# GpSimd sums x and the normalised rows at the end of layer 0's experts, where VectorE did it in layer 1's mix

## What is computed

```
x = x + experts0(layernorm(x))            # end of layer 0: the stage "mlp0"
xn = layernorm(x)
x = x + graph1(xn, edges) + mix1(xn)      # layer 1
# mix1: att = linear attention over xn (8 heads)
#       x1  = layernorm(xn + att @ Wo + bo)
#       out = layernorm(x1 + relu(x1 @ W1 + b1) @ W2 + b2)
# graph1(xn) ends with  "... + xn"
```

## Time and profile before

| what | value |
|---|---|
| time, median of 3 runs | 7430.36 us (7419.84 to 7437.67) |
| the profiled execution: its own time | 7422.03 us |
| its span | 7420.3 us |
| granted TensorE clock, mean | 0.906 of full speed |
| busy: TensorE / its weight loads / VectorE / ScalarE / GpSimd | 6067.1 / 4464.6 / 3771.2 / 2059.7 / 3528.7 us |
| mlp0 ends, context1 begins | at 3079.1 us of the span |
| mix1's loop | about 3560 to 5117 us of the span |

### The profile page before, as it was taken

One profiled execution on the slowest core, in us unless ns is written; L12 is line 12 of the kernel. 1 busy time (PEld: TensorE's weight loads), 2 busy tenths in 40 slices (PEclk: granted clock), 3 DMA queues, 4 the chain that ended last, 5 costly groups with the idle time before them and its releaser, 6 DMA issues. The chain is left out here.

```text
span 7420.3 us, 108117 instructions
## 1 busy us (share of the span) xinstructions
PE 6067.1 (82%) x27723; PEld 4464.6 (60%) x27724; DVE 3771.2 (51%) x10125; ACT 2059.7 (28%) x4653; POOL 3528.7 (48%) x3672
## 2 busy tenths in 40 slices
PE   6697888888887999766688888885789898896399
PEld 5454556666655777533566666664566666674287
DVE  6111115767665543353455545556566666677700
ACT  3023441000012444211122222221123445665121
POOL 1777776777773111477777777774200000001411
PEclk8898888999998999888788889887899999998699
DMA  7887776666662211578777777775688888665600
GB/s 249 290 266 235 232 238 200 199 200 199 196 196 65 44 60 63 158 225 240 241 245 244 246 250 246 247 246 153 220 254 256 253 255 247 197 204 175 209 31 18
DMA packets 783301, 1482.22 MB, mean 200 GB/s; under 512 B 315424, under 2 KB 545254, under 8 KB 713719
## 3 DMA queue, kind: packets, MB, share of 16 engines
q1 hardware_dynamic: 520060, 930.09, 38.6%
q0 software_dynamic: 168160, 451.64, 21.0%
q10 hardware_dynamic: 94790, 96.95, 4.0%
HBM read 970.15 MB, written 508.94 MB: 199 GB/s over the span
## 5 line engine op out<-in xcount | busy, mean ns | idle before, releaser
L759 POOL DMA_INDIRECT rows_ring<-h_rows,src_idx x1660 | 1569.6, 946 | 636.3 <-issue 485.9
L2115 POOL DMA_INDIRECT x_sb<-xn_rows,src_tile x1563 | 1549.8, 992 | 482.1 <-issue 475.2
L2951 PE MATMUL sums_ps_sum<-x_sb,sums_weighted 128*125 x4124 | 969.3, 388 | 133.9 <-DVE sums_weighted L2915 99.2
L2951 PEld LDWEIGHTS sums_ps_sum<-x_sb,sums_weighted 128*125 128x125 f32 x4124 | 744.2, 187 | 359.1 <-issue 254.4
L2915 DVE SCALAR_TENSOR_TENSOR sums_weighted<-x_sb 128x125 f32 x2062 | 720.0, 349 | 375.7 <-PE sums_ps_sum L2951 283.8
L902 PE MATMUL agg_ps_sum<-rows_ring,agg_sel_w 128*128 128x257 f32 x1820 | 546.7, 444 | 148.1 <-DMA rows_ring<-h_rows,src_idx 141.7
L2881 POOL DMA_INDIRECT node_tops<-tops,last_edge x98 | 94.5, 965 | 967.6 <-DMA x_sb<-row_lots 956.4
L870 DVE TENSOR_SCALAR agg_sel_w<-agg_ps_spots,dst_item,w_item 128x128 f32<-128x128 f32 x1660 | 542.5, 400 | 0.0
L902 PEld LDWEIGHTS agg_ps_sum<-rows_ring,agg_sel_w 128*128 128x128 f32 x1820 | 292.6, 202 | 278.9 <-issue 187.8
L902 PE MATMUL agg_ps_sum<-agg_rows,agg_sel_w 128*128 128x257 f32 x1500 | 419.3, 422 | 10.8 <-issue 10.4
L868 DVE TENSOR_TENSOR agg_sel<-agg_ps_spots,dst_item 128x1280 bf16<-128x1280 f32 x166 | 247.5, 1491 | 328.0 <-PE agg_ps_sum L903 328.0
(11 more groups left out here) (705 smaller groups left out, 10655.7 us busy)
## 6 DMA issues: line engine op xcount, KB each, us to landing
row_lots<-x_sb SPq DMA_DIRECT2D x195, 1048.0 KB
x_sb<-row_lots SPq DMA_DIRECT2D x195, 1048.0 KB
edge_rows<-rows_ring SPq DMA_DIRECT2D x75, 1290.0 KB
agg_rows<-edge_rows SPq DMA_DIRECT2D x75, 1290.0 KB
fin_z<-sums SPq DMA_DIRECT2D x97, 642.5 KB, 3.8
sums<-sums_z ACTq DMA_DIRECT2D x500, 112.4 KB, 5.9
rows_ring<-h_rows,src_idx POOLq DMA_INDIRECT x1660, 2.8
mix_xt<-xn_turned SPq DMA_DIRECT2D x100, 256.0 KB, 7.0
```

The costliest lines, as they stand in the source:

```text
L759: return pool.indirect_dma_start(self.ring[:, item // LOT_ROWS % LOT_RING, item % LOT_ROWS, :], None, self.table, bass.IndirectOffsetOnAxi ...
L2115: pool.indirect_dma_start(self.ring[:, s, i, :], None, g.xn_rows, bass.IndirectOffsetOnAxis(g.src_tile[:, tile:tile + 1], 0)).then_inc(sel ...
L2951: pe.matmul(ps[0:M, bass.ds(bank, SW)], weighted[:, s + j, :, :].rearrange("p n w -> p (n w)"), rows[:, bass.ds(off, SW)], start=False, st ...
```

## The change

GpSimd adds `xn2` to `x_sb` in place for each group, right after its copy of line 1612 and before the wait for `terms_kept`. The stores of x to `x_rows` now hold x + xn; each is issued after the row store of the tenth group of its set, and waits for GpSimd's add, so the fifth stands in the last slot, 56. ScalarE may write a buffer of `xn2` again only when GpSimd has read it. In mix1 the add of xx_part is gone; mlp_part waits for the load of `xx` itself; SP loads the next `xr` when `x1_ready` says that norm_part has used the old one, where it waited for `xx_added`.

```diff
@@ mlp0, SP
-                    if s % 10 == 0 and 0 < s <= GROUPS:
-                        sp.wait_ge(added, s)
-                        t = (s - 10) * GROUP
-                        sp.dma_start(x_to[:, t:t + 20, :], g.x_sb[:, t:t + 20, :]).then_inc(x_stored, 16)
                     b = s - BEHIND
                     if is_group(b):
...
                         sp.dma_start(g.xn_rows[b * ROWS:(b + 1) * ROWS, :].rearrange("(j p) c -> p j c", p=P), xn2[:, u, :, :]).then_inc(rows_out[u], 16)
+                        if (b + 1) % 10 == 0:
+                            sp.wait_ge(x_plus, b + 1)
+                            t = (b - 9) * GROUP
+                            sp.dma_start(x_to[:, t:t + 20, :], g.x_sb[:, t:t + 20, :]).then_inc(x_stored, 16)
@@ mlp0, GpSimd
                     pool.tensor_copy(xn2[:, u, :, XROW - 1:XROW].rearrange("p j o -> p (j o)"), g.dinv[:, b * GROUP:(b + 1) * GROUP]).then_inc(dinv_set, 1)
+                    pool.wait_ge(scaled2, b + 1)
+                    x = g.x_sb[:, b * GROUP:(b + 1) * GROUP, :]
+                    pool.tensor_tensor(x, x, xn2[:, u, :, 0:C], ALU.add).then_inc(x_plus, 1)
                     pool.wait_ge(terms_kept, b + 1)
@@ mlp0, ScalarE
                     if b >= RING2:
                         act.wait_ge(rows_out[b % RING2], 16 * (b // RING2))
+                        act.wait_ge(x_plus, b + 1 - RING2)
                     two.scale(act, g, xn2[:, b % RING2, :, :], b).then_inc(scaled2, 1)
@@ mix1, SP
                         sp.wait_ge(q_done, gi - 1)
-                        sp.wait_ge(xx_added, gi - 1)
+                        sp.wait_ge(x1_ready, gi - 1)
@@ mix1, VectorE
-                    dve.wait_ge(xx_added, gi + 1)
+                    dve.wait_ge(xx_loaded[u], k16)
                     dve.tensor_tensor(xx[:, u, :, :], xx[:, u, :, :], r[:, :, :], ALU.add).then_inc(added, 1)
-
-                def xx_part(gi, u, k16):
-                    dve.wait_ge(xx_loaded[u], k16)
-                    dve.tensor_tensor(xx[:, u, :, :], xx[:, u, :, :], xr[:, u, :, :], ALU.add).then_inc(xx_added, 1)
...
                         x1_part(gi, n)
-                        xx_part(gi, u, 16 * k + 16)
```

More of the change, by code:

```diff
@@ L1451, in mlp0 @@
         turned_out = [ph.sem(f"turned_out{u}") for u in range(RING2)]
-        x_stored, scattered = ph.sem("x_stored"), ph.sem("scattered")
+        x_stored, scattered, x_plus = ph.sem("x_stored"), ph.sem("scattered"), ph.sem("x_plus")
         one, two = BatchMoments(ph, "one"), BatchMoments(ph, "two")
@@ L2386, in mix1 @@
         loaded, rows_loaded = [S("loaded0"), S("loaded1")], [S("rows_loaded0"), S("rows_loaded1")]
-        xx_loaded, mixed_out, xx_added = [S("xx_loaded0"), S("xx_loaded1")], [S("mixed_out0"), S("mixed_out1")], S("xx_added")
+        xx_loaded, mixed_out = [S("xx_loaded0"), S("xx_loaded1")], [S("mixed_out0"), S("mixed_out1")]
         w_loaded, w_ready, bias_done, bias_ready, var_ready, root_ready = (
@@ L2656, in norm_part, with mlp_part @@
                     rows_norm(n, r, x1n, norms).then_inc(x1_ready, 1)
-                def mlp_part(gi, u, n, norms, x1_parts):
+                def mlp_part(gi, u, k16, n, norms, x1_parts):
                     dve.wait_ge(f_done, gi + 1)
@@ L2694, in body @@
                         if not start:
-                            mlp_part(gi - 1, 1 - u, n, 2 * gi + 1, gi + 1)
+                            mlp_part(gi - 1, 1 - u, 16 * k + 16 * u, n, 2 * gi + 1, gi + 1)
                         x1_part(gi, n)
-                        xx_part(gi, u, 16 * k + 16)
                 peeled(dve, PAIRS, body)
                 n = Count(GROUPS * OWN + (GROUPS - 1) * MLP)
-                mlp_part(GROUPS - 1, 1, n, 2 * GROUPS, GROUPS)
+                mlp_part(GROUPS - 1, 1, 16 * PAIRS, n, 2 * GROUPS, GROUPS)
 def attention(nc, g):
```

## The result

The changed kernel takes 7448.86 us at the median of 8 runs (7437.16 to 7453.01), the kernel before 7428.44 us (7419.84 to 7437.67) beside it: ratio 1.0025, 95% interval 1.0015 to 1.0036. The forecast was 7425 us with a range of 7410 to 7437. So the change costs 0.25%, some 19 us by that ratio, where 5 were to be gained.

The account below looks back on a forecast made before the run. TensorE was taken to bound mlp0's loop, GpSimd's gathers narrowly mix1. Terms +3 (mlp0's end), +0 (its loop), -8 (mix1) gave -5 us: 7417 against the profiled execution, 7425 for the median, range 7410 to 7437.

Parts of the forecast that it names:

- The add on GpSimd in mlp0 ... Cost 0: In mlp0's loop, GpSimd's added 72 us fit in its 493 us idle; cost 0, or 14.4 us without cover.
- the sum that had only touched stages in it: Whole kernel: +3 for mlp0's end, +0 for its loop, -8 for mix1, together -5 us.
- mlp0's loop +0.: mlp0's loop keeps TensorE's pace, so the add on GpSimd there changes its time by 0 us.
- Rival C: GpSimd's add holds VectorE in mlp0's ten batch-opening slots: slower by 17 us or more, 7447; chance 0.04.
- The stage ends 3.3 us later ... I take 3.: End of mlp0: x's last store lands after GpSimd's drain, costing 3 us, bounds 1.4 to 5.6.
- mix1: I take 5.5, the share: In mix1, removing one of five VectorE instructions that stretch gathers saves 5.5 us, bounds 0 to 20.
- rival B: mix1 gains nothing because the gathers' excess stays, and mlp0's end costs: +3 us, 7433; chance 0.15.
- The rule of the Trainium skill: In mix1, one VectorE add could hold a gather for its full 0.69 us, 34 us in all; trace shows less.
- GpSimd's own waits ... 2.9 us.: In mix1, GpSimd's 6.6 us of waits for the ring of lots shrink by 2.9 us, bounds 0 and 6.6.
- 50 x 0.61 = 30.5 us is what a reader of this loop alone would expect: mix1's TensorE-VectorE loop: dropping the 0.61 us add from 50 groups would save 30.5 us, if read alone.
- TensorE waiting for `xt` in the end: In mix1, VectorE's savings beyond a few us become TensorE waits for `xt`; about 1 us in hand at the end.
- The end is GpSimd's, by a small margin.: mix1 ends with GpSimd's gathers; the last sum lay ready 2.5 us behind the lots in SP's list.

Follow-up runs that it names:

- a_noadd: Changed kernel without GpSimd's add in mlp0 and the waits for it; context0, mix0 and aggregate0 together take 1923.8 us.
- d1: Kernel before plus fifty one-number adds on GpSimd in mlp0, one per group; ratio 1.0007.
- b_same: The kernel before, unchanged, measured again in the first series; median 7429.02 us.
- m_mlp0: Changed mlp0 with the old mix1, its add on VectorE; layer 1's gathers at 946 ns span 2023.9 us.
- a_same: The changed kernel, unchanged, measured again in the first series; median 17.5 us above the kernel before.
- e_tinyxx: Changed mlp0 with the old mix1 lists, but xx_part adds a single number per row; context1 and mix1 take 2033.7 us, fin 472.5.
- d2_again: Kernel before plus one tiny GpSimd add in mlp0's last group, measured again in the fourth series; ratio .9983.
- a_again: The changed kernel, unchanged, measured again in the fourth series; median 16.4 us above the kernel before.
- c4_after50: Changed kernel plus fifty small writes (memsets) on GpSimd in mlp0; gather levels and time not moved.
- d3_vector: Changed kernel with mlp0's add on VectorE instead of GpSimd; ratio .9995 to the kernel before, mlp0 781.7 us.
- c1_mlp50: Kernel before plus fifty small writes (memsets) on GpSimd in mlp0, one per group; gather levels and time not moved.
- c2_end50: Kernel before plus fifty small writes (memsets) at the very end of GpSimd's list; gather levels and time not moved.
- b_again: The kernel before, unchanged, measured again in the fourth series; median 7438.01 us.
- d2_tiny1: Kernel before plus one tiny GpSimd add in mlp0's last group; ratio .9985 in the third series.
- d4_tinyend: Kernel before plus fifty tiny adds at the very end of GpSimd's list, behind all gathers; layer 0's gathers take 957 ns.
- c3: Kernel before plus 25 small writes (memsets) on GpSimd in mlp0, one every second group; gather levels and time not moved.

## Why the prediction was wrong, point by point

**"The add on GpSimd in mlp0 ... Cost 0" and the sum that had only touched stages in it.** This is the step that failed. The sum was made of mlp0 and mix1, -5 us, and these two came out at -3.9. It had no term for the stages ahead of and behind the diff, and they cost 21 us in the profiled pair: +12.9 in A, +4.2 in fin, and 3.8 in kmax, sums and pick, of which kmax and sums vary by more from run to run. In the pairs of series 1 and 4 A costs 15.6 and 16.2 us, fin 4.2 and 4.8, and the touched stages give back 11.0 and 12.2, with layer 1's gathers 7 and 8 ns shorter. Without the add A is back at 1923.8 us (a_noadd); with adds of one number it is not (d1, 1939.6). Layer 0's gathers take 957 or 960 ns in all eight profiles with fifty adds more in GpSimd's list, 946 or 949 in the eight without, and 949 in the two with one. So that the presence of these adds lengthens them is shown. Why it does is open.

**"mlp0's loop +0."** Right. TensorE is busy 583.8 of 584 us, it waits for nothing there in the profile after, and GpSimd's add is cheaper than thought: 1188 ns at the median (1177 to 1202), not the 1442 of norm_last's. What ran beside it differs: in mlp0 mostly VectorE's `mlp_h`, which reads PSUM (31.9 of the adds' 59 us), in norm_last `last_junk`, with two inputs in SBUF (54.7 of some 70 us). That this is the reason was not tested. Rival C did not come.

**"The stage ends 3.3 us later ... I take 3."** The mechanism was right: x's last store, not GpSimd's drain, ends the stage. Counted from mlp0's start, which moved by 14.2 us, GpSimd's last copy did not move at all (3068.59, 3082.76), the add ended at 3084.09, 1.3 us after the copy's start (2.1 us earlier than put, since no group was late), and the landing took 9.5 us, not 9.1. The whole stage: +1.7 us in the profiled pair, +0.1 in series 1, +4.4 in series 4.

**"mix1: I take 5.5, the share" of the gathers' excess.** Wrong, though the stage did get 5.6 us shorter. The excess over the median in mix1's window, worked out as for the earlier trace rows, is with the add on VectorE 26.8 (before), 29.4 (b_same) and 22.4 us (m_mlp0), without it 27.5 (after), 26.7 (a_same) and 28.6 (a_noadd). It does not fall. What fell is the level of every gather, 953 to 946 ns, 10.9 us, and 4.6 us of that came back as waits for the ring. So in what the add does to the gathers rival B was right, and the forecast's number came out by luck: the same two kernels give -11.1 us in series 1 and -16.6 in series 4. The rule of the Trainium skill that the prediction weighed ("SBUF — State Buffer", section "SBUF: two separate sides": GpSimd and VectorE exclude each other for a whole instruction) would, as it was applied there, make the excess fall with each add that goes; these windows show no fall at all. The page limits the case of a VectorE instruction with two SBUF inputs to a GpSimd operation that reads SBUF, and whether a gather counts as one no run here shows.

**"GpSimd's own waits ... 2.9 us."** Wrong in sign: 6.6 became 11.2 us (9.7 in b_same, 15.1 in a_same). The waits were 6.4 to 17.7 us in the six profiles at 953 ns and 11.2 to 17.8 in the five at 946; m_mlp0, with VectorE as before, waits 15.5 us. That a faster gather waits longer for the ring is suggested by this, not shown.

**"50 x 0.61 = 30.5 us is what a reader of this loop alone would expect", and TensorE waiting for `xt` in the end.** The 30.5 us did not even show up in the loop. TensorE waits 8.5 us less for `fq` and 6.5 more in `out`:

```profile
PE mix_ps_n L2491 <- DVE mix_fq L2640: 176.4, 49, 4.2
PE mix_ps_o L2501 <- DVE mix_at L2648: 51.3, 50, 4.9
...
PE mix_ps_q L2483 <- DMA mix_xt<-xn_turned: 0.6, 1, 0.6
```

(184.9 and 44.8 before). `xt` is late once, by 0.6 us. SP does not wait as forecast either: 245.1 us for gathers, where it was 277.3, and 655.4 for `added`, where it was 643.1. VectorE itself has new gaps, in its waits after, from 3606 to 5106 us:

```profile
DVE mix_mv L2617 <- DVE mix_st L2613: 17.1, 95, 0.5
DVE mix_qb L2633 <- DVE mix_x L2679: 12.9, 24, 0.6
```

The second did not exist before, and the first was 14.5. There are 24 gaps of 0.54 us, one for every second group: that is, for each pass of a loop whose body is a pair of groups. From the start of `mix_x` to that of the next `qb` it was 1.33 us in every group and is now 0.81 and 1.23 by turns, 14.9 us less over the 48 groups; the 2.6 us more before `mix_mv` take their part too. So VectorE itself keeps about half of the 30.5 us. It is not the missing instruction that makes the pause: in e_tinyxx, with an add of 0.16 us in that place, the two times are 0.82 and 1.25. So the pause shows where the work at that place is short; the add of 0.69 us seems to have covered it.

What VectorE saves does not shorten the loop. From the first `added` to the last it takes 1487.1 us, where it was 1493.7, but the granted clock in mix1's window went from 0.89 to 0.90 as well. Where that clock is alike (0.895 to 0.897) the loop takes 1493.8 (b_same), 1491.7 (m_mlp0) and 1491.5 us (d2_again) with the add, 1491.1 (a_same) and 1494.0 (a_again) without. Over all profiles it is 1488.0 to 1496.9 us with the add and 1479.0 to 1497.4 without. The waits for `xt` that the prediction saw coming are there in other profiles, and not only without the add: 46.1 us in c4_after50 and 97.6 in d3_vector, but also 15.1 in c1_mlp50, 23.3 in c2_end50 and 41.5 in b_again. In these five the last sum lies ready 9.9 to 10.6 us before the last lot is stored, so there the gathers hold the loop. In the other thirteen TensorE waits 3 us or less for `xt`.

**"The end is GpSimd's, by a small margin."** Right in all eight profiles at 953 ns and above, by 1.5 to 10.6 us. At 946 and 949 ns either chain can end it: the gathers by 1.2 us in after and by 10.4 in c4_after50, the last sum in m_mlp0 and in a_same (ready at 5129.87, the last lot stored at 5128.23).

**The range.** Its upper end, 7437, was the worst run of the kernel before. The forecast's own range, 7412 to 7434, does not follow from its terms: +1.4 - 18 and +5.6 + 0 around 7430.4 give 7414 to 7436. More than these 2 us it lacked a term for what an edit does to a program of 108,000 instructions as a whole; here that was up to 11 ns on each of 1660 and up to 8 on each of 1563 serial instructions, 18 and 13 us and of opposite sign.

**Is there a better kernel?** d2_tiny1, the kernel before with one add more that does nothing, was faster in both series, .9985 and .9983 (intervals above), with layer 1's gathers at 949 ns where the kernel before had 957 in series 4 (in series 3 it was not profiled). Its medians, 7427.80 and 7424.19 us, are also what the kernel before reached in series 1 and 2. So this is the kernel before at a luckier level, not a design.

## What to carry to other kernels

When a stage is a chain of thousands of equal instructions, compare the median and the minimum of one of them in every stage, the untouched ones too, before reading the stage that was edited: a step of 1% there outweighs most edits. Build the edit's parts as dummies as well (the instruction at a size of one number, at another place, or one that does nothing): they tell what the edit's work does from what its presence does. And time taken from a loop's critical run is not a gain until the gaps of the engine itself are counted again: here half of it came back as a pause that had not shown before. Where two profiles of a stage are compared, compare their granted clocks too, and take more than one profile of each before reading a difference of 5 us in 1500.

## What the runs showed of the hardware that was not expected

- Gathers on GpSimd stand at levels: 946, 949, 953, 957 and 960 ns at the median, each held through a stage of some 1600 instructions, the minimum 4 to 8 ns under it. Two stages of one program can have different ones, and they change with instructions that run only later (d4_tinyend: fifty adds behind the last gather, 946 to 957 in layer 0). Small writes in the same places change nothing (c1 to c3). The same program stood 3 to 4 ns higher in a later series on the same chip. What sets them is open: whether it is the program's image or what the execution before left was not tried.
- A GpSimd add of 128 x 512 numbers took 1188 ns in mlp0 (1177 to 1202) and 1442 at the median in norm_last of the same profile (1259 to 1470).
- VectorE can pause 3.7 to 4.1 us, four times in fin, with nothing shown that ends it; this goes with the instructions in its list of an earlier stage (472.5 us in e_tinyxx, 476.4 to 478.2 without that instruction). d3_vector, which has fifty more in mlp0, shows no such pause and no wait for ScalarE in that place either, and has the shortest fin, 467.2. The mechanism is open.
- In the changed kernel VectorE paused 0.54 us once for each pass of mix1's loop (24 times) after its last instruction there, and 0.13 us in the other groups. With an add of 0.69 us more at that place no pause is seen, with one of 0.16 us the times from `mix_x` to `qb` are as without it.
